# Latent attention: exponentials turned unscaled, context multiplied by reciprocal sums that TensorE spreads, a new plan and four query slots

## The reference

```python
q = einsum('bld,dhk->blhk', x_bld, Wq)                 # B=4, L=1024, D=256, 16 heads of 64
latent = einsum('bld,dc->blc', x_bld, Wkv_down)        # 64 wide
k, v = (einsum('blc,chk->blhk', latent, W) for W in (Wk_up, Wv_up))
attn = softmax(where(causal, einsum('bqhd,bkhd->bhqk', q, k) / 8, min), axis=-1)
out = einsum('bqhd,hdo->bqo', einsum('bhqk,bkhd->bqhd', attn, v), Wout)
```

## Time and profile before

| | before |
|---|---|
| time, median of 3 runs (lowest, highest) | 2357.19 us (2355.04, 2358.47) |
| span of the profiled execution, first to last instruction | 2344.6 us |
| stage with the change, from its first instruction at 1346.8 us | some 998 us |
| TensorE clock granted, mean | 0.944 |
| busy shares of the span, PE / DVE / ACT / POOL | 88% / 73% / 56% / 61% |

### The profile page before, as it was taken

One profiled execution on the slowest core, in us unless ns is written; L12 is line 12 of the kernel. 1 busy time (PEld: TensorE's weight loads), 2 busy tenths in 40 slices (PEclk: granted clock), 3 DMA queues, 4 the chain that ended last, 5 costly groups with the idle time before them and its releaser, 6 DMA issues. The chain is left out here.

```text
span 2344.6 us, 44938 instructions
## 1 busy us (share of the span) xinstructions
PE 2056.7 (88%) x15232; PEld 1599.0 (68%) x15232; DVE 1714.9 (73%) x3132; ACT 1310.0 (56%) x3178; POOL 1436.5 (61%) x1209
## 2 busy tenths in 40 slices
PE   6579999999899999999999679899889988998885
PEld 4467777777677777777777466677567756775764
DVE  5587777777767887677675278787879787977783
ACT  3346566766566567666674265455545554555541
POOL 2475666656665576566663158676767676767673
PEclk8789999999999999999999889999999999999998
DMA  8343333333333433333322137686768676867676
GB/s 285 89 99 87 87 94 93 83 91 87 95 82 94 115 86 78 83 89 91 88 66 73 73 94 171 163 201 155 188 166 198 159 189 165 197 162 175 165 183 145
DMA packets 191582, 298.16 MB, mean 127 GB/s; under 512 B 52264, under 2 KB 97660, under 8 KB 190332
## 3 DMA queue, kind: packets, MB, share of 16 engines
q1 hardware_dynamic: 179068, 271.17, 45.8%
q10 hardware_dynamic: 12288, 24.13, 4.1%
HBM read 56.04 MB, written 20.97 MB: 33 GB/s over the span
## 5 line engine op out<-in xcount | busy, mean ns | idle before, releaser
L2024 POOL TENSOR_TENSOR g_pt<-g_pt,g_rl 128x1024 f32<-128x1024 f32 (+2 forms) x112 | 292.7, 2625 | 137.5 <-DVE g_rl L1960 133.0
L1744 PE MATMUL ps<-g_turned,g_latV 128*64 128x256 f32 (+1 forms) x1984 | 309.3, 458 | 69.0 <-issue 48.6
L854 ACT ACTIVATE l_pp<-ps,l_mx 128x256 f32<-128x256 f32 (+1 forms) x512 | 228.4, 463 | 167.4 <-DVE l_mx L991 167.4
L2024 POOL TENSOR_TENSOR g_pp<-g_pp,g_rl 128x768 f32<-128x768 f32 (+3 forms) x112 | 238.6, 2138 | 103.1 <-DVE g_rl L1960 102.6
L1130 POOL TENSOR_TENSOR l_pp<-l_pp,l_rl 128x1024 f32<-128x1024 f32 (+1 forms) x128 | 230.1, 1798 | 86.4 <-DVE l_rl L999 86.4
L1744 PEld LDWEIGHTS ps<-g_turned,g_latV 128*64 128x64 f32 x1984 | 154.5, 149 | 156.7 <-issue 95.3
L1848 ACT ACTIVATE g_pt<-ps,g_mx 128x256 f32<-128x256 f32 (+3 forms) x256 | 200.6, 796 | 101.9 <-DVE g_mx L1942 47.8
L1848 ACT ACTIVATE g_pp<-ps,g_mx 128x128 f32<-128x128 f32 (+3 forms) x256 | 173.5, 693 | 142.6 <-DVE g_mx L1942 58.1
L1972 DVE STREAM_TRANSPOSE g_bt<-g_pt 128x1024 f32<-128x1024 f32 (+1 forms) x176 | 193.4, 1127 | 45.3 <-DMA g_turned<-g_bt 24.5
L1147 POOL TENSOR_TENSOR l_act_lo<-l_u,l_act_hi 114x512 fp32r<-114x512 f32 x96 | 125.8, 1310 | 161.9 <-ACT l_act_hi L904 161.7
L991 DVE CUSTOM_DVE_ANT_0 ps<-ps,l_mask 128x256 f32<-128x256 f32 (+1 forms) x512 | 188.4, 441 | 7.3 <-PE ps L703 7.3
(11 more groups left out here) (199 smaller groups left out, 6061.8 us busy)
## 6 DMA issues: line engine op xcount, KB each, us to landing
l_pt<-l_bt SPq DMA_DIRECT2D x1024, 64.0 KB, 2.0
g_turned<-g_bt SPq DMA_DIRECT2D x320, 128.0 KB, 3.1
g_turned<-g_bt SPq DMA_DIRECT2D x320, 96.0 KB, 2.2
g_turned<-g_bt SPq DMA_DIRECT2D x224, 112.0 KB, 2.8
g_turned<-g_bt SPq DMA_DIRECT2D x224, 80.0 KB, 2.1
l_tab<-turns SPq DMA_DIRECT2D x64, 128.0 KB, 2.2
g_turned<-g_bt ACTq DMA_DIRECT2D x64, 128.0 KB, 4.2
g_turned<-g_bt SPq DMA_DIRECT2D x96, 64.0 KB, 2.1
```

Source lines behind the costliest of these rows:

```text
L854: act.activation(PP[:, i % NP, at, 0:n], ps[:, bank + a, jj * 2 * P:jj * 2 * P + n], ACT.Exp, bias=mx[:, g % 2, h, at:at + 1], scale=-1.0, ...
L1744: last = pe.matmul(o, latV[:, b % 2, c, :], turned[:, :, a, c, :, :], start=(c == 0), stop=(c == t), skip_group_check=True)
L2024: pool.tensor_tensor(view, view, rl[:, u % 2, mine(k):mine(k) + n].unsqueeze(2).to_broadcast([P, n, keys(u)]), ALU.mult).then_inc(s["scale ...
```

## The change

`scale` is gone. `blocks` turns the exponentials as ACT wrote them, and waits only for `exp`. `share` is one reciprocal for a whole unit (96 instead of 224), and waits until `weigh` of two units earlier is done (`pv`). The factor is brought in after `weigh`: ahead of each unit's `weigh`, TensorE multiplies the reciprocals (one column, repeated to 64) with the identity, so that the reciprocal of query row q stands in all 64 rows of its head in PSUM beside the context: one 128x64 by 128x128 matmul for each head, 512 in all. For units of eight heads the two halves take two neighbouring PSUM banks. `evacuate` copies context and factors, twice the columns. `divide` begins with a multiplication of the two in SBUF. `g_ctxu` grows to twice its size, and the ring of queries loses a slot (`QS` 5 to 4). `COST`, `RANK`, `cost` and `needs` have new entries, so every queue of the stage is in a new order. The number of DMAs is the same.

```diff
-QS = 5
+QS = 4
...
-    COST = (3.471, 3.519, 2.419, 3.062, 4.333, 5.048, 2.885, 5.766)
+    COST = (4.571, 3.923, 2.011, 2.809, 4.828, 5.535, 2.542, 5.643)
...
-        "pool": {"split_x": -30.64, "scale": -27.92, "divide": 13.5},
+        "pool": {"split_x": -49.69, "divide": 23.65},
...
+        if event[0] == "weigh" and self.size(event[1]) == 8:
+            runs = [r for r in ((i, i + 1) for i in range(7)) if late(r) is not None]
+            return min(runs, key=lambda r: (late(r), -r[0])) if runs else None
...
                         pe.wait_ge(s["v"], tile(u)[0] + 1)
+                        pe.wait_ge(s["rl"], u + 1)
+                        n = plan.size(u) // 2
+                        for h in range(2 * n):
+                            at = bank * CH + (n + h // 2) * P
+                            pe.matmul(flat[64 * (h % 2):64 * (h % 2) + 64, at:at + P], rl[:, u % 2, h:h + 1].to_broadcast([P, DH]),
+                                      ident[:, :], start=True, stop=True, skip_group_check=True)
...
-                    n = plan.size(u) // 2 * P
-                    act.activation(ctxu[:, u % NCU, 0:n], ps[:, bank, 0:n], ACT.Copy).then_inc(s["ev"], 1)
+                    n = plan.size(u) * P
+                    act.activation(ctxu[:, u % NCU, 0:n], flat[:, bank * CH:bank * CH + n], ACT.Copy).then_inc(s["ev"], 1)
...
-                def share(k):
-                    u, p = pairs[k]
-                    dve.wait_ge(s["ex"], heads[k + 1])
-                    if u >= 2 and p == 0:
-                        dve.wait_ge(s["scaled"], first[u - 1])
-                    own = slice(mine(k), mine(k) + plan.wide(units[u][1]))
+                def share(u):
+                    dve.wait_ge(s["ex"], heads[first[u + 1]])
+                    if u >= 2:
+                        dve.wait_ge(s["pv"], u - 1)
+                    own = slice(0, plan.size(u))
                     dve.reciprocal(rl[:, u % 2, own], sm[:, u % 2, own]).then_inc(s["rl"], 1)
...
-                    dve.wait_ge(s["scaled"], k + 1)
+                    dve.wait_ge(s["ex"], heads[k] + a + n)
...
-                def scale(k):
-
-                    u, p = pairs[k]
-                    pool.wait_ge(s["rl"], k + 1)
-                    n = plan.wide(units[u][1])
-                    view = probs(k, 0, n).rearrange("p (a n) -> p a n", a=n)
-                    pool.tensor_tensor(view, view, rl[:, u % 2, mine(k):mine(k) + n].unsqueeze(2).to_broadcast([P, n, keys(u)]),
-                                       ALU.mult).then_inc(s["scaled"], 1)
-
...
                     pool.wait_ge(s["ev"], u + 1)
+                    pool.tensor_tensor(view, view, part, ALU.mult).then_inc(s["scaled"], 1)
+                    pool.wait_ge(s["scaled"], u + 1)
```

60 lines of the change are left out of this document (30 added, 30 removed).

## The result

The changed kernel takes 2394.11 us (median of 4 runs, 2381.4 to 2401.14) against 2356.11 us for the kernel before in the same runs: a ratio of 1.0154, 95% interval [1.0126, 1.0183]. It is slower by 38 us; the forecast was 2351, its range ended at 2388.

A forecast was written before the change was run, and what follows sets the result against it. The prediction took SP's queue of DMA issues plus its waits to bound the kernel. Its terms, -20.0 + 10.8 + 3.0 - 1.2 + 1.4 = -6.0, added to the median 2357.2, gave 2351 us; the range was 2320 to 2388.

The forecast's parts named there:

- What bounds the stage: SP's queue: the stage takes SP's issuing, 914.1 of 956.9 us, plus its waits of 42.8 us.
- TensorE's rival: TensorE paces, so each unit's spreading lengthens the stretch: 2366 to 2381, up to 2408, most likely 2375; chance 0.24.
- Scale gone, -20.0: Without `scale` on POOL, SP's waits for transposes mostly go: -20.0 us, bounds 0 and 25.8.
- Loads of x, +10.8: SP's queue: seven adjacent stores and loads of x instead of three, 2.7 us each: +10.8, bounds 0 and 14.
- Spreading, +3.0: TensorE's 60.8 us of added matmuls mostly fit its idle time; only SP's waits for `weigh` grow: +3.0, bounds 0 and 7.6.
- The order taken at nothing but for the loads of x: Second bank and lost query slot can hold back scores, which run three units ahead: taken at 0, bounds 0 and +5.
- The query slot at 0 to +5: The fourth query slot gone, bounded together with the second bank: may hold back scores, 0 to +5 us, taken at 0.
- Head and tail, -1.2 and +1.4: First unit loses a `scale` and a reciprocal, -1.2; behind the last move come spreading, longer copy and multiplication, +1.4.
- Copies and products at nothing: ACT's copies grow by 27 us and POOL's products take 88 us where 531 left: counted at nothing.
- The new wait on VectorE: `share` waits for `weigh` of u-2, holding transposes behind it and SP's next move: 2365 to 2380; chance 0.04.
- The main case's range: The forecast's own case, 2351 us with its terms' bounds, was given as 2340 to 2362; chance 0.42.
- The case with `scale` hidden anyway: SP's 25.8 us of transpose waits stay: 2371, or 2357 if loads of x hide in them; chance 0.11.

The follow-up runs named there:

- e10: The changed kernel, same instructions, with COST and RANK searched anew by the planner's own estimate: 2348.9 us, ratio 0.9976 to the kernel before.
- e13: e10 without the spreading matmuls, ScalarE copying the context twice in their place (context not divided): 2350.95 us, ratio 0.9965 to the kernel before.
- e1: The kernel before, own order, with 512 matmuls of the spreading's shape ahead of `weigh`, their output overwritten: 2380.11 us against 2357.96, ratio 1.0083.
- e2: The changed kernel, own order, without the spreading matmuls, ScalarE copying the context twice instead (context not divided): 2384.52 us, ratio 1.0117 to the kernel before.
- e16: The changed kernel with a second searched order (COST and RANK), from another start of the search: 2369.18 us, ratio 1.0065 to the kernel before.
- e17: The changed kernel with a third searched order (COST and RANK), again from another start: 2370.77 us, ratio 1.0066 to the kernel before.
- e6: The kernel before with four query slots instead of five, its own costs and ranks: 2399.4 us against 2360.36, ratio 1.0162.
- e9: The kernel before with four query slots, COST and RANK searched anew for them: 2372.2 us, ratio 1.0061 to the kernel before.
- e18: The kernel before with four query slots, in a second searched order: 2371.42 us, ratio 1.0078 to the kernel before.
- e14: The kernel before, five query slots and `scale` kept, with COST and RANK searched anew: 2351.74 us, ratio 0.9986 to the kernel before.
- e4: The changed kernel, same order, with the spreading ahead of TensorE's wait for the move's landing: 2392.09 us, ratio 1.0141 to the kernel before.
- e7: The changed kernel, same order, with four buffers of reciprocals instead of two: 2392.55 us, ratio 1.0127 to the kernel before.
- e8: The changed kernel, own order, without spreading, doubled copy or multiplication (context undivided): 2380.76 us, ratio 1.0086 to the kernel before.

## Why the prediction was wrong

**What bounds the stage: right.** SP's issuing is the same in all kernels within 2%, and the difference of the spans is made of its waits. TensorE's rival would have given a time near the measured one for a wrong reason: the same TensorE work fits into 45 us less (e10), and taking the spreading's 61 us (59 by the measured 0.058 us a record) out of e10 changes nothing that can be told (e13).

**Scale gone, -20.0: mis-sized.** SP's wait for transposes fell by 10.6 us, not 20. Its bounds held.

**Loads of x, +10.8: right.** Seven places instead of three, 18.6 us instead of 8.1: +10.5. The 2.7 us a place are no constant, though: e10's three cost 4.2 each.

**Spreading, +3.0: failed.** 0.058 us a record is as forecast. The step that failed is "It fits into each, barely in the first and the last. So the greater part is taken at nothing". Idle time of an engine that works through a fixed order is not room: here, in the orders of before and of the change, it lay at places where the next step in the queue was not ready, and the spreading stood at other places. It cost 22 us in the order of before (e1), some 10 in the change's (e2, with intervals that overlap), and nothing that can be told in e10's (e13). I had bounded it at 7.6.

**The order taken at nothing but for the loads of x: failed, and this is the greater part.** "The second bank of a unit of eight heads, and the fourth query slot gone, can hold back scores; the scores run some three units ahead, which covers a delay of a few us. I bound this at 0 and +5 and take 0." This looked only at scores that come late. What came late was `weigh`, and SP waits for it: +28.4 us, forecast at +3. The working named the fact that SP's move of u needs `weigh` of u-2, and counted it only at the four places of before, although the new order had moved `weigh` everywhere. That this is order and not work is shown by e10, e16 and e17 (same instructions, 23 to 45 us back).

What in the order does it is shown only in part. It is not simply how far the scores run ahead. By the plans they are 4.2, 4.0, 3.8, 3.8, 3.5 and 3.0 units ahead of `weigh` of units 24 to 29 in the change, where before has 4.5, 4.5, 4.2, 3.8, 3.2 and 3.0, so that they run further ahead than before at one unit only. e10 has 4.2, 3.5, 3.5, 2.8, 2.8 and 3.0, but e17, which is 23 us faster than the change as well, has 4.2, 4.0, 3.8, 3.8, 3.8 and 3.5. One part is the second bank: it held back not scores but a query part, behind an evacuation that stood late in ScalarE's queue, 12.5 us of TensorE's time at the three places named above, and a lower clock behind the one that was looked at. In e10 it costs nothing to speak of, so it is a price of this order and not of two banks. How SP's 28.4 us are shared between this and the rest of what stands ahead of `weigh` stays open.

**The query slot at 0 to +5: not right, in its order.** Four slots cost the kernel before 39 us in the order made for five (e6), and 14 and 18 us when searched anew (e9, e18), where five slots searched anew gained 5 (e14). How much of the 38 us is the change's own missing slot can't be said: the change with five slots wasn't tried.

**Head and tail, -1.2 and +1.4.** Measured +0.6 and +3.4. The first move starts at 1368.8 us in the change and at 1385.8 in e4, whose order and work up to there are the same, so the head's term can't be tested at this size. Nor can the tail's: with the order of the change it takes 22.9 us in the change, 23.1 in e4 and 25.3 in e7, against 19.5 before.

**Copies and products at nothing: right as far as can be told.** 4 to 7 us together, with intervals that overlap (e8 beside e2). The fewer reciprocals were not tested by themselves. **The new wait on VectorE: costs nothing that can be told** (e7), as its low chance said.

**The main case's range was too narrow for its own terms.** The bounds as they stand in the prediction (0 to -25.8, 0 to 14, 0 to 7.6, 0 to 5, and 0.2 for head and tail) add up to 2332 to 2384, not 2340 to 2362. Even 2384 lies below the 2394 measured, so the miss is in the terms and not in the adding.

The case with `scale` hidden anyway was half right in its mechanism, and 2371 would have been too low all the same. No rival had the one that came: `weigh` later than its landing through what the plan puts ahead of it on TensorE, and through what that work waits for.

What stays open is whether the mechanism is worth anything for itself. At its best order it equals the kernel before at its best (0.9976 [0.9953, 1.0000] and 0.9986 [0.9965, 1.0007]); at its two other searched orders it equals the old mechanism at four slots. Orders from one search differ by 20 us among themselves, more than the mechanisms do. e10 has the lowest median of those that divide their context, at the edge of what can be told from the kernel before.
